# Attention and gated FFN in one kernel: matrix work in 64-row tiles, PSUM as four two-bank places, eight slots for exponentials

## The reference, cut to what matters

```python
x = layernorm(x + attn(x)); x = layernorm(x + ffn(x))       # x: 4 x 1024 x 128, fp32
# attn: 16 heads of 64, scale 1/8, Wq, Wkv 128 -> 1024 each, Wo 1024 -> 128
s = einsum('bhid,bhjd->bhij', q * scale, k)
gm = max(s, axis=-1)                                         # over the whole row, masked part too
p = where(causal_mask, 0.0, exp(s - gm))
out = einsum('bhij,bhjd->bhid', p, v) / (sum(p) + EPS)
return out @ Wo + bo
# ffn: r = sigmoid(mix_r @ W_r.T); k = relu(mix_k @ W_k.T) ** 2; out = r * (k @ W_v.T)
#      mix_* blends x with x shifted by one token
```

## Time and profile before

| | |
|---|---|
| time, median of three runs | 1086.66 us (1086.21 to 1087.02) |
| the profiled execution, first to last instruction | 1084.1 us |
| the profiled execution's own time beside its span | the page gives the span alone; the median lies 2.6 us above it |
| PE matmuls busy | 1033.0 us, 95% |
| VectorE busy | 915.7 us, 84% |
| ScalarE busy | 745.6 us, 69% |
| GpSimd busy | 582.8 us, 54% |
| 16 DMA engines, mean | about half busy |

### The profile page before, as it was taken

The page is one execution under the profiler, slowest core; times in us unless marked ns, Lnnn a source line. Parts: engine busy times, 40 slices in busy tenths (PEclk is TensorE's granted clock), DMA queues, the critical chain, the costliest instruction groups (busy, mean ns, idle before and its releaser), DMA issues. The chain is left out here.

```text
span 1084.1 us, 22071 instructions
## 1 busy us (share of the span) xinstructions
PE 1033.0 (95%) x7427; PEld 675.5 (62%) x7427; DVE 915.7 (84%) x1546; ACT 745.6 (69%) x1709; POOL 582.8 (54%) x918
## 2 busy tenths in 40 slices
PE   7899999999999999999999999999999999999895
PEld 5566666666666666666666666666666666666563
DVE  5988888988888888888889888888988888898967
ACT  5667667666676666676676667667666766766777
POOL 5355655555565455556555556655555565554364
PEclk9999999999999999999999999999999999999998
DMA  5255565445556545555654455565445556554542
GB/s 163 57 126 130 129 146 125 117 107 129 133 125 147 119 110 119 127 127 133 147 126 113 108 128 127 133 148 124 114 111 126 132 127 147 122 123 113 118 113 78
DMA packets 74209, 134.07 MB, mean 124 GB/s; under 512 B 26864, under 2 KB 36848, under 8 KB 74096
## 3 DMA queue, kind: packets, MB, share of 16 engines
q1 hardware_dynamic: 73520, 132.26, 51.6%
q10 hardware_dynamic: 576, 0.39, 0.2%
HBM read 21.17 MB, written 2.36 MB: 22 GB/s over the span
## 5 line engine op out<-in xcount | busy, mean ns | idle before, releaser
L746 DVE TENSOR_SCALAR_CACHE_REDUCE tile<-ps_s 128x1024 f32<-128x1024 f32 x512 | 608.5, 1222 | 137.7 <-PE ps_s L984 132.2
L576 ACT ACTIVATE tile<-tile,neg_max 128x640 f32<-128x640 f32 (+7 forms) x512 | 396.2, 774 | 206.7 <-POOL tile L407 206.4
L984 PE MATMUL ps_s<-ks,qs 64*128 64x512 f32 x3072 | 425.9, 409 | 6.0 <-DVE tile L746 4.0
L407 POOL TENSOR_SCALAR_AFFINE_SELECT tile<-tile 128x128 f32<-128x128 f32 x512 | 149.6, 293 | 449.3 <-DVE tile L746 446.9
L984 PEld LDWEIGHTS ps_s<-ks,qs 64*128 64x128 f32 x3072 | 269.7, 185 | 125.9 <-issue 61.7
L1038 PE MATMUL ps_x<-pt,vs 128*64 128x256 f32 (+1 forms) x2560 | 270.2, 361 | 1.1 <-issue 1.1
L755 DVE STREAM_TRANSPOSE stage<-tile 128x640 f32<-128x640 f32 (+3 forms) x256 | 255.2, 1025 | 0.0
L1038 PEld LDWEIGHTS ps_x<-pt,vs 128*64 128x64 f32 x2560 | 175.0, 137 | 107.9 <-issue 35.8
L997 PE MATMUL ps_x<-ident,tile 128*128 128x128 f32 x640 | 117.3, 290 | 22.6 <-ACT pt L624 11.9
L997 PEld LDWEIGHTS ps_x<-ident,tile 128*128 128x128 f32 x640 | 69.1, 140 | 103.2 <-issue 51.8
L918 PE MATMUL ps_x<-xs,ws 128*128 128x512 f32 x381 | 119.0, 421 | 0.1
(11 more groups left out here) (92 smaller groups left out, 576.7 us busy)
## 6 DMA issues: line engine op xcount, KB each, us to landing
pt<-stage SPq DMA_DIRECT2D x512, 120.0 KB, 2.5
pt<-stage SPq DMA_DIRECT2D x512, 88.0 KB, 2.1
rb<-recips SPq DMA_DIRECT2D x64, 256.0 KB, 4.1
y<-in_L_attn_x SPq DMA_DIRECT2D x3, 512.0 KB, 8.2
out<-y SPq DMA_DIRECT2D x3, 512.0 KB, 3.2
pt<-in_L_attn_Wkv SPq DMA_DIRECT2D x2, 384.0 KB, 6.7
pt<-in_L_attn_x SPq DMA_DIRECT2D x2, 256.0 KB, 4.6
wos<-in_L_attn_Wo SPq DMA_DIRECT2D x1, 512.0 KB, 7.2
```

The source lines that it names most:

```text
L407: pool.affine_select(out=block_of, in_=block_of, compare_op=ALU.is_ge, fill=fill, base=0, pattern=[[-1, P]], channel_multiplier=1).then_in ...
L576: act.activation(cols, cols, ACT.Exp, bias=neg_max[:, at:at + 1], scale=-1.0, accum_out=sums[:, p % 2, a, t:t + 1]).then_inc(s_exp, 1)
L746: dve.tensor_scalar(tile[:, at, :], ps_s[scores_at(p, t, a)][:, :], -SCALE, None, ALU.mult, ALU.min, accum_out=neg_max[:, at:at + 1]).then ...
L984: ins = mm(ps_s[scores_at(p, t, a)][:, c * HALF:(c + 1) * HALF], qs[rows, p % 2, qh, t * P:(t + 1) * P], ks[rows, p % 2, kh, c * HALF:(c + ...
```

## The change

All work of PE but P*V now runs in tiles of 64 rows. A projection over 128 channels is cut in the lower and the upper 64, `rows`. `across` pairs them: in the first half of the block the low rows write bank 0 of the place and the high rows bank 1, and in the second half it is the other way round, adding up. Between the halves PE waits for its own first half (`s_side`), since both would write the same bank. A transpose takes 64 of the 128 rows of the tile, so there are twice as many, each with 64 columns, the low rows into one bank and the high ones into the other. The number of columns in all of these pairs of matmuls is as before.

PSUM is four equal places of two banks. A table `FOLLOWS` says after whose user each user takes its place, and `released` waits for that one's evacuation. q, k, v and the output projection come in one block a pair each with one ACT copy of 1024 columns (before: two copies of 512); tiles 0 and 1 share a group of transposes (`turn_group`, `take_group`). `tile` has 8 slots, four query tiles; `ot` is doubled, `full_k` is a whole 1024 columns; SBUF for it comes from `dynamic_dma_scratch_size=1024`. P*V parts 2 and 1 of the pair before now follow each other behind the last score block. The lists of ACT, DVE, POOL and SP are reordered, and the first part of the tail's POOL list is longer.

```diff
-RING = 6
+RING = 8
+FOLLOWS = {
+    ("scores", 0, 1,): (("scores", 7, 1,), 1),
+    ("scores", 3, 0,): (("scores", 2, 0,), 0),
+    ("scores", 3, 1,): (("out",), 2),
+    ("scores", 4, 0,): (("scores", 3, 0,), 0),
+    ("scores", 4, 1,): (("group", 0,), 0),
+    ("scores", 5, 0,): (("scores", 3, 1,), 0),
+    ("scores", 5, 1,): (("k",), -1),
+    ("scores", 6, 0,): (("group", 1,), 0),
+    ("scores", 6, 1,): (("scores", 5, 0,), 0),
+    ("k",): (("v",), 1),
+    ("group", 0,): (("scores", 2, 1,), 0),
+    ("group", 1,): (("scores", 4, 0,), 0),
+    ("group", 2,): (("scores", 4, 1,), 0),
+    ("pv", 0,): (("scores", 5, 1,), 0),
...
-        ps_s = [psum(f"ps_s{n}", [P, N]) for n in range(NSCORES)]
-        ps_x = [psum(f"ps_x{n}", [P, HALF]) for n in range(NSHARED)]
+        places = [psum(f"ps{n}", [P, N]) for n in range(NPLACES)]
...
-                q, u = (p, t - 3) if t >= 3 else (p - 1, t + TILES - 3)
+                back = RING // 2
+                q, u = (p, t - back) if t >= back else (p - 1, t + TILES - back)
...
+            low, high = slice(0, DH), slice(DH, P)
+            across = (((low, 0), (high, 1)), ((high, 0), (low, 1)))
+
+            def turn_group(p, g):
+                place = place_for(("group", p, g))
+                drained(("group", p, g))
+                pe.wait_ge(s_exp, SLOTS * p + 2 * GROUPS[g][-1] + 2)
+                n = 0
+                for a in range(2):
+                    for t in GROUPS[g]:
+                        for j in range(t + 1):
+                            for h, rows in enumerate((low, high)):
+                                out_cols = place[:, h * HALF:(h + 1) * HALF].rearrange("p (q c) -> p q c", q=2)
+                                ins = turn(out_cols[:, :, n * 32:n * 32 + 32],
+                                           tile[rows, slot_of(p, t, a), j * P:(j + 1) * P], ident[rows, rows])
+                            n += 1
+                ins.then_inc(s_group, 1)
+
+            def project_qk(p, what, n):
...
+                    drained((what, p))
+                else:
+                    pe.wait_ge(s_side[what], p)
+                for m, (wh, xh) in enumerate(terms):
+                    for rows, c in across[n]:
+                        cols = slice(c * HALF, (c + 1) * HALF)
+                        ins = mm(place[:, cols], ws[rows, "qk".index(what), wh, r * P:(r + 1) * P],
+                                 xs[rows, b % XSLOTS, xh, cols], start=(n == 0 and m == 0), stop=(n == 1 and m == 2))
+                ins.then_inc(s_side[what] if n == 0 else s_proj[what], 1)
...
-    nc = bacc.Bacc("TRN2", target_bir_lowering=False, num_devices=1)
+    nc = bacc.Bacc("TRN2", target_bir_lowering=False, num_devices=1, dynamic_dma_scratch_size=1024)
```

More of the change, by code:

```diff
@@ L35 @@
 BLOCKWISE = range(TILES // 2, TILES)
[L37 to L43, removed]
+GROUPS = ((0, 1), (2,), (3,))
+GROUP_OF = {t: g for g, tiles in enumerate(GROUPS) for t in tiles}
+NGROUPS = len(GROUPS)
 QK0 = [("q", 0), ("k", 0), ("k", 1), ("q", 1)]
[L45 to L52, removed]
 LAST = ALL_PAIRS - 1
@@ L107 @@
[L107 to L112, removed]
+NPLACES = 4
+ORDER = [
+    ("scores", 0, 0, 0),
+    ("scores", 0, 1, 0),
+    ("q", -1),
+    ("scores", 1, 0, 0),
+    ("scores", 1, 1, 0),
+    ("out", 2),
+    ("scores", 2, 0, 0),
+    ("scores", 2, 1, 0),
+    ("v", 0),
+    ("scores", 3, 0, 0),
+    ("scores", 3, 1, 0),
+    ("group", 0, 0),
+    ("k", -1),
+    ("scores", 4, 0, 0),
+    ("scores", 4, 1, 0),
+    ("scores", 5, 0, 0),
+    ("scores", 5, 1, 0),
+    ("group", 1, 0),
+    ("group", 2, 0),
+    ("scores", 6, 0, 0),
+    ("scores", 6, 1, 0),
+    ("pv", 0, 0),
+    ("scores", 7, 0, 0),
+    ("scores", 7, 1, 0),
+    ("pv", 2, 1),
+    ("pv", 1, 1),
+]
@@ new lines, in is_real, with places_of_users @@
+def is_real(user):
+    kind, p = user[0:2]
+    return 1 <= p <= ALL_PAIRS if kind in ("q", "k") else 0 <= p < ALL_PAIRS
+def places_of_users():
+    place, before, users = {}, {}, []
+    fresh = 0
+    for k in range(-4, ALL_PAIRS):
+        for kind, *rest, back in ORDER:
+            user = (kind, k - back, *rest)
+            (kind2, *rest2), ago = FOLLOWS[(kind, *rest)]
+            past = (kind2, user[1] - ago, *rest2)
+            if past in place:
+                place[user] = place[past]
+                before[user] = past if is_real(past) else before.get(past)
+            else:
+                place[user] = fresh
+                fresh += 1
+            users.append(user)
+    assert fresh == NPLACES
+    first = [place["scores", 0, 0, 0], place["scores", 0, 0, 1]]
+    names = first + [n for n in range(NPLACES) if n not in first]
+    return {user: names.index(n) for user, n in place.items() if is_real(user)}, before, [u for u in users if is_real(u)]
@@ L205, in build @@
         s_lo0 = sem("s_lo0")
-        s_proj = sem("s_proj")
-        s_full = sem("s_full")
+        s_proj = {what: sem(f"s_proj_{what}") for what in "qk"}
+        s_full = {what: sem(f"s_full_{what}") for what in "qk"}
         s_qkhi = sem("s_qkhi")
@@ L216, in build @@
         s_turned = sem("s_turned")
-        s_quad = sem("s_quad")
+        s_group = sem("s_group")
+        s_side = {what: sem(f"s_side_{what}") for what in ("q", "k", "v", "out")}
         s_pt = sem("s_pt")
@@ L266, in build @@
         normed = [tokens(y[:, b * N:(b + 1) * N]) for b in range(B)]
-        gate = [tokens(tile[:, n, :]) for n in (2, 3)]
+        gate = [tokens(tile[:, n, :]) for n in GATE_SLOTS]
         def sums_of(b, t):
```

752 lines of the change are left out of this document (466 added, 286 removed).

## The result

The changed kernel takes 1099.03 us (median of four runs, 1096.77 to 1099.74), the kernel before beside it 1086.54 (1086.21 to 1087.02). The ratio is 1.011, interval 1.0096 to 1.0125: slower by 1.1%. Forecast were 1040 us, faster by 4.3%, and a range from 1016 to 1072. The measured time lies above the range, and on the other side of the kernel before.

The account below looks back on a forecast made before the run. The prediction took PE's work and waits, 31.42 us a pair, to set the period. Streaming 26.6, switches 0.7, self-waits 1.4, other waits 1.1 and 0.15 gave 29.9 a pair, hence 1040 us, range 1016 to 1072.

Parts of the forecast that it names:

- Rest: The prediction's list of remaining items, among them DMAs, x halves, ACT's larger copies and the tail, all taken as costing nothing.
- The x halves: Six turns of an x half stay in 128*128 tiles between P*V blocks, two switches each as before: no cost.
- The clean pair: The period of a pair was summed to 29.9 us instead of 31.4.
- the term for P*V: PE's streaming time for P*V in a pair, taken as 7.5 us of the 26.6 of streaming.
- The tail: Up to three more POOL steps before the first square, against fewer switches in the last pair: zero, +-3.
- A: Rival: PE's instruction supply limits the doubled loads and matmuls; +3.4 us a pair, 1146 us; 12 in 100.
- B: Rival: matmuls alone, not loads, limited to one in 62 ns at most; +11 us; 5 in 100.
- C: Rival: more waits, ACT's copies or POOL's masks 0.5 to 1.4 us a pair late; 1056 to 1083 us; 15 in 100.
- S3, k and tile 5: Places where rival C could add waits: score block of tile 3, k projection, tile 5's mask; three margins under 0.4 us.
- the wait for VectorE ahead of tile 6: PE's score block of tile 6 waits for DVE's third evacuation, 18.6 instead of 17.7: loss 1.0 us a pair.
- Four self-waits: PE waits for itself between the halves of q, k, v and output, 0.35 us each: loss 1.4 a pair.
- A switch: PE switching between 64*128 and 128*128 tiles costs 0.20 us; 0.7 instead of 3.1 a pair, gain 2.4.

Follow-up runs that it names:

- e1: The changed kernel with P*V parts 1 and 2 exchanged, part 1 now ahead of part 2 behind the last score block: 1073.3 us, ratio 0.9875.
- e2 to e4: Four more small DMAs a pair on SyncE's queue: in the changed kernel 1190.1 us, in e1 1077.6, in the kernel before 1088.0, one run each.
- e5: e1 with VectorE's subtraction of x's low half moved ahead of the two evacuations of the first score tile: 1060.5 us, ratio 0.9753 to the kernel before.
- e6: The changed kernel with VectorE's subtraction of x's low half moved ahead of the first score tile's evacuations, P*V order kept: 1089.5 us, ratio 1.0022.
- e8: e5 with the transposes of tiles 0 to 3 in 128-row tiles again, 20 a pair of 128 columns: 1072.8 us, ratio 0.9864 to the kernel before.
- e11: e5 with VectorE's, ScalarE's and GpSimd's steps of the last pair and the tail reordered: 1054.5 us, ratio 0.9701 to the kernel before.

## Why the prediction was wrong

**The step that failed** is in *Rest*: "DMAs are the same in number and bytes, issued in other places; parts 2 and 1 of P*V are a pair late, so they are covered by more than 10 us." The number is right, the cover is not. I looked from the data to its use, and the age of the pair said 10 us. The region that the data goes to is free only when the part of P*V that reads it last is through, and the change put that part at the very end of PE's pair, with the part that needs the last transfer just ahead of it. Between the two lie 35 issues, 22 us of SyncE, which I never priced: no row of SyncE's queue stands in my rows. What the runs showed in place of a covered transfer is a closed loop: P*V part 1, 35 issues, the last landing, P*V parts 2 and 1. 31.81-31.01 = 0.80 a pair is its net cost, 24.8 us, shown by e1 from one side and by e2 to e4 from the other; with the 5.3 us that e1 pays for its own order it is about 30. The Trainium skill says under "DMA: Bandwidth & Descriptors", section "Issuing engines are not separate DMA queues", that the sequencer time to initiate a DMA "is usually small relative to the DMA itself". The trace does not bear that out for these pieces of 88 to 120 KB: 0.65 a piece on one queue against 2.1 to 2.9 from issue to landing, a quarter to a third of it, and the landings overlap each other while the issues add up.

**The x halves, a second failure of the same line of Rest**: "The six turns of an x half stay in 128*128 tiles between P*V blocks, at two switches each as before; nothing." The turns did stay (so not quite all of PE's work but P*V is in 64-row tiles), but their subtraction on VectorE became the release of a score place. 0.55 a pair, 17.1 us, shown by e5 over e1. Taken away first, with the loop still there (e6), it gives 9.5 us.

**The clean pair**: forecast 29.9, measured in e5 30.33 to 30.37. +0.45 over 31 pairs is 14 us. In e5 tile 4 starts at 13.5 (forecast 13.4), tile 6 at 18.85 (18.6), the last two parts of P*V at 24.33 (23.1 and the 1.1 of the wait: 24.2). So 0.13 has come up by then, and 0.3 is in these two parts, 6.0 long where the sum left 5.7. Two things make most of the 0.45. One is the wait for ScalarE between the parts, 0.2 in most pairs, some 5 us; it belongs to the swap and not to the change. The other is the term for P*V, 7.5 in the sum. The blocks of the kernel before that my rows leave out:

```profile
541.74 2.60 PE L1038 MATMUL ps_x<-pt,vs 128*64 128x256 f32 x24
544.27 1.66 PE L984 MATMUL ps_s<-ks,qs 64*128 64x512 f32 x12
545.86 3.46 PE L1038 MATMUL ps_x<-pt,vs 128*64 128x256 f32 x32
```

From start to start the three blocks take 2.31, 2.53 and 3.39, with 0.21 ahead of each 8.9, and less the 1.1 that the prediction gives to their six switches 7.8: the term was 0.3 too small, 9 us.

**The tail**, taken as 0 +-3: +5.3.

Together 24.8+17.1+14+5.3 = 61. The profiled span is 1097.9 where the forecast has 1037, which is 61 as well; the medians, 1099 and 1040, are 59 apart.

**What held.** A is refuted: 40 transposes in 64-row tiles are quicker than 20 of before. 12 of them go by in 0.48 us, 40 ns each with its load, and v's 24 matmuls take 1.75 with their self-wait (529.64 to 531.39), as summed. The group of transposes:

```profile
L1169 PE MATMUL ps<-ident,tile 64*128 64x64 f32 x1280 | 58.0, 224 | 9.1 <-DVE tile L874 9.1
```

B is refuted with it. The Trainium skill gives under "TensorE: Matmul & The Clock Gate", section "Wait — 56ns, not 53.3ns?", about 62 ns a matmul for decoding in the sequencer's own code; at 40 ns each these transposes show that this bound does not hold here. C was right in kind, more waits, but not where it looked: S3, k and tile 5 came within 0.3 us of the walk. Of the steps, the wait for VectorE ahead of tile 6 was forecast at 1.0 and measures 0.52, with 0.3 more ahead of the second block of transposes. Four self-waits are there with 0.3 each, but their removal brings a loss. A switch is about 0.12 by e8 and not 0.20; for twelve fewer that is 1.5 a pair and not 2.4, and part of what lacks is made up by the quick transposes (40 at 0.04 are 1.6, where 2.2 was summed). That the clean period still came within 0.45 of the forecast is in part luck, since these errors are of both signs. Without the two failures the change is what it was forecast to be in sign: e5 has it at -2.5% and e11, with the tail in order, at -3.0%, where -4.3% was forecast.

What stays open: why single issues of SyncE take 0.9 to 2.2 us, and why the clock fell after the x wait in four of six pairs of e1 and in none of the changed kernel's, whose wait is as long.

## What to carry to other kernels

When a reader of a buffer is moved to the end of the period, follow the circle: who may refill it only then, how long the refiller's queue takes in issues, and who needs the last piece; a transfer that is "a pair late" is covered only as far as its target is free. Price a DMA queue like an engine, issues times their duration, even where it has never been waited for. And before a wait or a block is taken out of a tuned order, ask what it covers: splitting four blocks in halves with other work between cost 80 us here, one step of VectorE 30.

## What the runs showed of the hardware

An issue on SyncE takes 0.59 us (median of 1139), in a row 0.62 to 0.67 each, with some 4 to 5% of them at 0.9 to 3.4. Pairs of 64-row transposes cost 0.08 us for 128 columns, where a full-array transpose of 128 columns took 0.11. A wait of PE of 1.6 to 2.7 us was in some places followed by a stretch mostly at the lower of the two levels, 1.2 GHz: the mean granted clock of the 4 us behind the wait was 0.57 or 0.58 in four pairs of e1_swap and 0.60 and 0.63 in pairs 23 and 30 of the changed kernel. In others of the same length it stayed at 1.00, such as the six waits of 1.64 to 1.66 for the x halves in the changed kernel. A score block in such a stretch took 2.77 to 2.93 us instead of 1.65.
